# All level outputs of a turn in one group of products on 64 columns of the array each, second source tiles, and a new order of four engines

## What is computed

```python
def step(carry, xs):
    Sk, Sv = carry
    q_t, k_t, v_t, w_t, g_t, b_t = xs
    gt = jnp.exp(g_t)
    bw = b_t[:, :, None] * w_t
    Sk = Sk * gt[:, :, None, :] + k_t[..., :, None] * bw[:, :, None, :]
    Sv = Sv * gt[..., None] + bw[..., None] * v_t[:, :, None, :]
    s = jnp.einsum('bhd,bhdm->bhm', q_t, Sk) * SCALE
    a = jax.nn.softmax(s, axis=-1)
    o_t = jnp.einsum('bhm,bhmd->bhd', a, Sv)
    return ((Sk, Sv), o_t)
...
q = short_conv(h @ Wq, cq)      # k, v, w in the same way; w is l2-normed per head
g = jax.nn.log_sigmoid(h @ Wf1 @ Wf2)
...
o = o * jax.lax.rsqrt(jnp.mean(o * o, axis=-1, keepdims=True) + EPS)
o = o * norm_w * jax.nn.sigmoid(gate)
return o.reshape(o.shape[0], o.shape[1], -1) @ Wo
```

## Time and profile before

| | |
|---|---|
| median of 3 runs (lowest to highest) | 2795.52 us (2793.87 to 2795.84) |
| the profiled execution, its time | 2791.86 us |
| its span in the trace | 2790.1 us |
| busy: PE, PEld, DVE, ACT, POOL | 98%, 68%, 81%, 58%, 51% of the span |
| granted TensorE clock, mean | 0.997 |

### The profile page before, as it was taken

How to read it: one execution, slowest core, us unless ns; L and a number is a source line. 1 busy time by engine, 2 the same in 40 slices (tenths; PEclk the granted TensorE clock), 3 DMA queues, 4 the chain that set the end, 5 groups by cost and what they waited for, 6 DMA issues and landing times. The chain is left out here.

```text
span 2790.1 us, 42861 instructions
## 1 busy us (share of the span) xinstructions
PE 2741.3 (98%) x13558; PEld 1910.1 (68%) x13558; DVE 2247.3 (81%) x5841; ACT 1629.7 (58%) x3649; POOL 1420.1 (51%) x2122
## 2 busy tenths in 40 slices
PE   6999899999999999999999999999999999999999
PEld 5888566666666666666666666666666666666887
DVE  7554689988888999888889998888898999884543
ACT  5111676677666666776666767666766666661110
POOL 0200366666666666665666666656666666661000
PEclk9999999999999999999999999999999999999999
DMA  4500211111112111111121111111211111105000
GB/s 170 196 16 16 79 35 36 35 50 35 49 35 65 55 61 35 50 35 50 35 73 50 58 35 50 35 50 35 80 50 58 35 51 37 50 29 193 16 16 31
DMA packets 90929, 151.03 MB, mean 54 GB/s; under 512 B 9296, under 2 KB 30928, under 8 KB 90192
## 3 DMA queue, kind: packets, MB, share of 16 engines
q1 hardware_dynamic: 90704, 148.29, 16.7%
HBM read 127.02 MB, written 21.23 MB: 53 GB/s over the span
## 5 line engine op out<-in xcount | busy, mean ns | idle before, releaser
L946 POOL TENSOR_TENSOR s<-s,tmp 128x256 f32<-128x256 f32 (+1 forms) x448 | 358.8, 801 | 312.0 <-DVE tmp L1258 276.1
L1611 PE MATMUL ps<-rows_even,standing 128*128 128x512 f32 x1024 | 498.1, 595 | 2.7 <-ACTq L1062 2.7
L1611 PE MATMUL ps<-hT,standing 128*128 128x512 f32 x1024 | 497.4, 593 | 0.0
L946 POOL TENSOR_TENSOR X<-S,D 128x256 f32<-128x256 f32 x384 | 278.8, 726 | 97.2 <-ACT S L1121 73.2
L1654 PEld LDWEIGHTS ps<-Y,S 128*128 128x128 f32 x1536 | 221.3, 191 | 153.1 <-issue 135.5
L946 POOL TENSOR_TENSOR Y<-aT,D 128x256 f32<-128x256 f32 x384 | 280.3, 751 | 0.0
L341 ACT ACTIVATE sig<-up_ps 128x512 f32<-128x512 f32 x88 | 52.6, 597 | 389.8 <-PE up_ps L570 389.8
L946 POOL TENSOR_TENSOR A<-ident,dg 128x512 f32<-128x512 f32 x64 | 66.7, 1041 | 380.3 <-DVE standing L1348 356.9
L1642 PEld LDWEIGHTS ps<-AM,XT 128*128 128x128 f32 x1536 | 211.6, 191 | 64.1 <-issue 60.2
L1258 DVE TENSOR_TENSOR tmp<-ps,D 128x256 f32<-128x256 f32 (+1 forms) x448 | 196.2, 438 | 63.7 <-PE ps L1642 47.6
L1587 PE MATMUL ps<-standing,og 128*128 128x512 f32 x480 | 245.2, 593 | 0.0
(11 more groups left out here) (215 smaller groups left out, 6679.5 us busy)
## 6 DMA issues: line engine op xcount, KB each, us to landing
standing<-in_wk_dram SPq DMA_DIRECT2D x64, 256.0 KB, 2.5
standing<-in_ww_dram SPq DMA_DIRECT2D x64, 256.0 KB, 2.6
standing<-in_wq_dram SPq DMA_DIRECT2D x64, 256.0 KB, 2.7
standing<-in_wv_dram SPq DMA_DIRECT2D x64, 256.0 KB, 2.8
standing<-in_wo_dram SPq DMA_DIRECT2D x64, 256.0 KB, 3.3
wq_dram<-wq SPq DMA_DIRECT2D x3, 2816.0 KB, 20.0
space<-in_w_dram SPq DMA_DIRECT2D x8, 704.0 KB, 11.1
x_sb<-in_x_dram SPq DMA_DIRECT2D x4, 1024.0 KB, 5.6
```

What stands on the lines that cost most here:

```text
L946: return nc.gpsimd.tensor_tensor(out, in0, in1, op)
L1611: mm = nc.tensor.matmul(bank[x][:, :], ck_(slot[x], kk), hT[n // NH % 2][:, kk, :], start=(kk == 0), stop=(kk == KT - 1))
```

## The change

`outputs(l)` is cut in two again: four products per level instead of two, each with 64 columns of the stationary tile and 64 moving columns, whose results land on partitions 0 to 63 or 64 to 127. The sources of one half meet only targets of the same half, so the rest of the old 128 x 128 result, which the mask threw away, is not made. The levels' results get halves of four banks (0, 1, 5 and 6). `S[1]`, `S[2]`, `S[4]`, `S[8]` get a second tile, used by turns. All levels stand in one group behind `v3`, and all four engines' orders are changed. The silus of two halves become two calls that can stand apart. In turn 0 two transposes of the identity fill the upper part of bank 5.

```diff
+TWICE = (1, 2, 4, 8)
+def rows_pat(t, p0, p1, at, *dims):
+    part = t[p0:p1, :]
+    return bass.AP(part.tensor, part.offset + at, [list(part.ap[0])] + [list(d) for d in dims])
+
+def target_half(t, l, i, j, rows=(0, P)):
+    if l == 64:
+        return rows_pat(t, *rows, j * P + i * (P // 2), (1, P // 2))
+    return rows_pat(t, *rows, i * (P // 2) + j * (P // 4), (P, 2), (1, P // 4))
+
+def odd_target_half(t, i, j):
+    return pat(t, 1 + i * P + j * (P // 2), (HALF - 1, 2), (2, P // 4))
...
-        S = {l: sb(f"S{l}", [P, HALF]) for l in LEVELS}
+        S = [{l: sb(f"S{l}", [P, HALF]) for l in LEVELS}]
+        S += [S[0] | {l: sb(f"S{l}b", [P, HALF]) for l in TWICE}]
...
+        for l, (i, half) in {1: (0, 0), 2: (0, 1), 4: (1, 0), 8: (1, 1), 16: (5, 0), 32: (5, 1), 64: (6, 0)}.items():
+            bank[f"a2_{l}"] = psum[i][:, half * HALF:(half + 1) * HALF]
...
                 def outputs(l, done):
                     for i in range(2):
-                        last = nc.tensor.matmul(pair_columns(bank[f"a2_{l}"], i), ck_(S[l], i),
-                                                odd_targets(aT, i) if l == 1 else pair_columns(Y[l], i),
-                                                start=True, stop=True)
+                        for j in range(2):
+                            half = (j * (P // 2), (j + 1) * (P // 2))
+                            last = nc.tensor.matmul(target_half(bank[f"a2_{l}"], l, i, j, half),
+                                                    ck_(S[u % 2][l], i)[:, half[0]:half[1]],
+                                                    odd_target_half(aT, i, j) if l == 1 else target_half(Y[l], l, i, j),
+                                                    start=True, stop=True)
                     last.then_inc(done, 1)
```

More of the change, by code:

```diff
@@ L629, in _ @@
             down_tile(NB - 1, MT - 1)
[L632 to L635, removed]
+PE_EARLY = "k w g q wT v x2T kT A x4T vT x8T x16T x32T gate x64T s4 xbT s0 s2 s8 U2 U0 U1".split()
+PE_LATE = "s16 s32 skT sst s64 sT aT a2_1 a2_2 a2_4 a2_8 a2_16 a2_32 a2_64 o onT".split()
+ACT_EARLY = ("acc_k acc_w g acc_q h2 we w x h4 sq xe xt0 k c2 acc_v ke h8 c4 h16 qe q c8 h32 c16 ve v c32 xt2 h64 "
+             "xt4 c64 xt8 h128 xt16 xt32 xt64 xtb St0").split()
 ACT_LATE = "sk sg e0 e1 e2 e3 aT osq".split()
[L637 to L641, removed]
+DVE_EARLY = ("ck1 ck2 ck3 cw1 cw2 cw3 p2 cq1 cq2 p4 cq3 p8 ss cv1 p16 cv2 p32 cv3 kr As p64 at0 at1 am1 at3 am4 vr "
+             "am2 am8 p128 am16 m2 m1 at2 m4 am32 St1 m8 St2").split()
+DVE_LATE = ("m16 am64 m32 mst m64 sx0 sx1 sx2 sx3 mx nms dg0 dg1 dg2 dg3 rs a2_1 a2_2 a2_4 a2_8 a2_16 a2_32 a2_64 "
+            "oss on oge og").split()
+POOL_EARLY = "b1 bne b2 bnp b4 bn b8 b16 b32 b64 x1 zero ad2 ad4".split()
 POOL_LATE = "ad8 ad16 ad32 adst ad64 a2d y2 y4 y8 r1 y16 y32 y64 yst r2 r3 r4 r5".split()
+TWICE = (1, 2, 4, 8)
 BLOCK = [0, 2, 1, 3]
@@ L1036, in turn @@
                     tt(r2[:, :], r1[:, :], oss[:, :]).then_inc(pool_late, 1)
+                if early:
+                    pool.wait_ge(act_early, after(ACT_EARLY, "c32", n))
+                    decay_sources(32)
+                if late:
                     pool.wait_ge(pool_late, after(POOL_LATE, "r2", u))
                     tt(r3[:, :], r2[:, :], rms_eps[:, :], ALU.add).then_inc(pool_late, 1)
+                if early:
+                    pool.wait_ge(act_early, after(ACT_EARLY, "c64", n))
+                    pool.wait_ge(dve_early, after(DVE_EARLY, "p64", n))
+                    decay_sources(64)
+                if late:
                     pool.wait_ge(pool_late, after(POOL_LATE, "r3", u))
@@ L1466, in turn @@
                 if early:
-                    dve.wait_ge(dve_early, after(DVE_EARLY, "p4", n))
-                    decays(4)
+                    dve.wait_ge(act_early, after(ACT_EARLY, "acc_v", n))
+                    conv("v", 1)
                     dve.wait_ge(act_early, after(ACT_EARLY, "h8", n))
@@ L1628, in transpose_sources, with transpose_into_upper @@
                 def transpose_sources(l, done):
-                    transpose(f"x{l}T", lambda i: ck_(S[l], i), done, 2)
+                    transpose(f"x{l}T", lambda i: ck_(S[n % 2][l], i), done, 2)
+                def transpose_into_upper(into):
+                    for c in range(2, C):
+                        nc.tensor.transpose(ck_(into, c), ident[:, :], ident[:, :])
                 def chunk_scores(done):
@@ L1783, in turn @@
                     transpose_sources(2, pe_early)
+                if u >= C:
+                    out_rows(u - C, bank["out"], 1)
+                if early:
                     pe.wait_ge(dve_early, after(DVE_EARLY, "cq3", n))
-                    pe.wait_ge(act_early, after(ACT_EARLY, "k", n))
+                    pe.wait_ge(act_early, after(ACT_EARLY, "ke", n))
                     transpose("kT", lambda c: ck_(k, c), pe_early, C - 1)
-                    pe.wait_ge(act_early, after(ACT_EARLY, "q", n))
-                    chunk_scores(pe_early)
                 if late:
```

397 lines of the change are left out of this document (186 added, 211 removed), and 6 rows, old and new, of the table bank.

## The result

The changed kernel takes 2931.1 us (median of 4 runs, 2930.2 to 2932.2), the kernel before 2794.7 (4 runs beside it, 2793.6 to 2795.8): ratio 1.0488, 95% interval 1.047 to 1.0507. It is slower, as forecast, but by 136 us, not by 39; the time lies outside the range of 2806 to 2876. The profiled execution has a span of 2930.0 us at a mean granted clock of 0.995, so its rows can be set against that time directly.

The account below looks back on a forecast made before the run. TensorE was taken to bound the 34.14 us turn, with a chain across engines near 33.9; 0.55 + 0.03 + 0.07 = 0.65 us a turn gave plus 39 us, 2831, set at 2833 us; range 2806 to 2876.

Parts of the forecast that it names:

- the side-by-side case: TensorE's level products: both array halves work at once, 0.22 us a level, group 1.6 us.
- rivals 1 and 2: TensorE's products: halves follow one another, 2852 to 2874 us, chance 0.20; no gain from narrow instructions, 2990 us, chance 0.04.
- The seven merges: VectorE's chain of predicated copies behind ss, each waiting for the one before: 4.2 us, done at 967.49.
- Rivals 3 and 4: Wait at chunk_outputs absent, TensorE the bound, 2696 or 2767 us, chance 0.10; merges without latency, +4 us, chance 0.04.
- The start of the merges: VectorE's first merge, expected at 963.3 once p8 (0.9 us) and ss (0.6 us) are done.
- The rest of the turn: From chunk_outputs to the next au: 0.03 us for moved rows and 0.07 for small waits, otherwise nothing added.
- both meetings: TensorE's s4 waits for VectorE's vr, about 974.2, and U0 for on, 976.7; both were said to fit.
- 0.07 taken out of bounds of 0 to 0.4: Small TensorE waits at s4 and U0 per turn, taken low at 0.07 us, upper bound 0.4.
- 0.03 for the moved rows: On TensorE, A (0.89 us) moves behind chunk_outputs and one output row (0.86) ahead: +0.03 us a turn.
- VectorE's busy time unchanged: A sign to check in the changed kernel's profile, beside TensorE's busy time falling by some 60 to 100 us.

Follow-up runs that it names:

- run 3: Changed kernel with two 128-column products per level again, in the new place and order: 2946.0 us, ratio 1.0548.
- run 5: Run 1's kernel with VectorE's residual row, am4 and vr put ahead of am1, at0, at1 and at3: 2850.0 us, ratio 1.0201.
- Run 1: Changed kernel with GpSimd's level-1 source product moved forward to behind yst: 2887.9 us, ratio 1.0341.
- run 6: Kernel before with two useless GpSimd products, reading and writing SBUF, added beside am2: 2804.5 us.
- run 7: Kernel before with four useless GpSimd memsets, only writing SBUF, added beside am2: 2794.2 us.
- run 8: Run 5's kernel with A and the third output row also put ahead of chunk_outputs on TensorE: 2835.4 us, ratio 1.0148.
- run 9: Run 8's kernel without the merges of levels 8 and 16, whose outputs are left out of the result: 2829.8 us, ratio 1.0128.
- run 10: Run 8's kernel with ScalarE copies moved ahead of osq, and TensorE and VectorE operations reordered: 2841.3 us, ratio 1.0167.
- run 4: Kernel before with only the narrow 64-column products, each level in its old place: 2823.2 us, ratio 1.0108.
- run 2: Changed kernel with A and the third output row moved ahead of chunk_outputs into TensorE's wait: 2926.4 us, ratio 1.0477.

## Why the prediction was off

**Right.** The direction. The products take the time of the side-by-side case: 0.235 us a level, the group from 1038.20 to 1039.98, 1.78 us with entry and exit, against 1.6 forecast; rivals 1 and 2 are out. The group starts 7.84 us behind `au` (7.76). The seven merges stand in one piece, 1038.94 to about 1043.1, 4.2 us as worked out. TensorE waits for the last of them: 1.75 us between slots (1041.45 to 1043.20), 2.1 forecast, the difference being mostly the longer group. `chunk_outputs` comes 0.63 us later (0.55). The 1.36 us saved on TensorE end in that wait; run 3 gives them as worth 0.25. The clock stayed at 1.00 from 430 to 2450 us. Rivals 3 and 4 are out with the wait and the 4.2 us of the merges.

**Right in part by luck.** The start of the merges, 8.58 us behind `au` against 8.51 forecast, did not come from where I had it. `p8` held VectorE for 0.36 us and not 0.9, and `p4` for 0.83 and not 0.55; then `ss` waited 0.26 us for ScalarE's `sq`, and the first merge for TensorE's level 2 (run 3), which I had put 0.1 us sooner than VectorE.

**The step that failed** is "The rest of the turn". It said that both meetings, `s4` with `vr` and `U0` with `on`, "fit with nothing to spare", with 0.07 us taken out of bounds of 0 to 0.4, and 0.03 for the moved rows. Measured: 1.52 us. The sum for `vr` was made of durations that VectorE's operations had in the old order, 0.34 for the masked and 0.21 for the diagonal scores. In the new order they fall beside GpSimd's products, and the same instructions with the same operands take up to 0.69 us more. From the last merge to `on` I had 8.94 us (start to start) and it took 10.35; run 5, with these stretches gone, took 9.12. So the instructions and their order were counted rightly, and their lengths were wrong. Run 1 (one neighbour moved: 0.69 us a turn back) and run 5 (0.53 more) take 1.22 of the 2.05 us away without removing any work, and runs 6 and 7 show the cause in the kernel before, where products that read stretch `am2` and memsets do not. What is left, 0.83 us a turn and 2850 us, is 0.63 at `chunk_outputs`, 0.30 and -0.10, against 0.65 forecast. Of the 0.30, 0.22 is the `U` products' wait for `on`, and part of it stood in my own terms: 967.49 + 8.5 + 0.68 + 0.16 is 976.83 and not the 976.7 that I wrote, and for `vr` I left out the handover of 0.16 that I had counted for `on`.

**It stood in the rows.** The earlier trace rows show two `D` operations in 1.32 us, one of which takes 0.42 a little later; I used that 0.9 for `p8` as its length, and did not ask why one operation has two lengths. GpSimd's timeline has a product beside it, 966.08 to 966.81. The bound of 0.4 took in late arrivals only. A bound for "these seven operations meet a GpSimd read" could be had from the same row: up to 0.5 us each.

**"VectorE's busy time unchanged"** was a check of my own, and the first line to fail: 104 us more.

**What stays open.** Why the new order doesn't get below some 34.7 us a turn. Filling the long wait gave 0.22 (run 8), two merges less were worth 0.1 (run 9), and the changed queue of ScalarE lost 0.1 (run 10); each time the next of several chains of nearly the same length took over. No run separates them further. Nor was it tried to measure the 0.32 us of a change of form apart from its surroundings; it comes from a sum over run 4.

## What to carry to other kernels

When an order is changed, the lengths of VectorE's operations with two SBUF inputs belong to the old order: lay GpSimd's new timeline beside VectorE's, and put operations that read PSUM, or GpSimd's writes and idle time, where the two meet. After a change, compare busy time at equal instruction counts before looking at waits: the 1.59 us wait was the most visible row, and filling it gave 5 us at most (run 2); the busy time told the cause, worth 81 us (run 5). And where chains are close in length, a saving is realised only when the next chain's release is moved with it: the narrow products lost 0.6% in one place and gained 0.3% with one projection moved.

## What was not expected of the hardware

- A VectorE product of 128x256 with two SBUF inputs takes 0.41 us with nothing of GpSimd's beside it and 0.73 to 1.10 beside a GpSimd product that reads SBUF; a diagonal score 0.29 and 0.71. GpSimd's own product is stretched as well, 0.92 us where it takes 0.65. An operation with a PSUM input keeps its 0.68 beside such a product (run 6), and GpSimd's memsets leave 0.41 as it is (run 7).
- A change from 128 to 64 columns and back costs TensorE about 0.32 us (an estimate from run 4), more than a level saves (0.21); the Trainium skill (TensorEngine Tiling (Array Packing), Key Properties) has that a change drains the engine. The runs show the price; that a drain is what takes the time, none of them shows.
- Four float32 products of 64 stationary and 64 moving columns (eight instructions) take 0.235 us, 0.029 an instruction, where two of 128 by 128 (four instructions) take 0.446: the time of two halves side by side.
